# Totals and gate scores in TensorE column groups, and constant products ahead of TensorE's waits

## The reference

```python
x = _layernorm(x + _L0_gnn_ref(x, edge_weight, src, dst, ...))    # message = max over incoming edges
x = _layernorm(x + _L1_gnn_ref(x, edge_attr_64, src, dst, ...))   # edge attention
```

```python
he = edge_features @ edge_fc_W + edge_fc_b
t = relu(einsum('ed,mdf->emf', he, rel_att_W1) + rel_att_b1)          # three relations m
g = sigmoid(einsum('emf,mf->em', t, rel_att_W2) + rel_att_b2)         # gate scores
alpha = _seg_softmax(sum(hs * hd, -1), dst, n)                        # e / sum of e by destination
beta = _seg_softmax(g, dst, n)
h_att = segment_sum(alpha[:, None] * s_att, dst) / kk                 # sums of rows hs, weighted by alpha
h_rel = segment_sum(einsum('em,emf->ef', beta, t_rel), dst) / mm      # and by each of three betas
```

## Time and profile before

| | us |
|---|---|
| timed runs, median of 3 | 2290.52 |
| lowest, highest | 2287.78, 2296.37 |
| span of the profiled execution | 2723.8 |
| TensorE busy in it | 1843.7 (68%) |
| GpSimd busy | 1639.6 (60%) |
| VectorE busy | 1328.7 (49%) |
| ScalarE busy | 1115.3 (41%) |

### The profile page before, as it was taken

One profiled execution on the slowest core, in us unless ns is written; L12 is line 12 of the kernel. 1 busy time (PEld: TensorE's weight loads), 2 busy tenths in 40 slices (PEclk: granted clock), 3 DMA queues, 4 the chain that ended last, 5 costly groups with the idle time before them and its releaser, 6 DMA issues. The chain is left out here.

```text
span 2723.8 us, 43235 instructions
## 1 busy us (share of the span) xinstructions
PE 1843.7 (68%) x9891; PEld 1146.6 (42%) x9891; DVE 1328.7 (49%) x5220; ACT 1115.3 (41%) x3305; POOL 1639.6 (60%) x1705
## 2 busy tenths in 40 slices
PE   4577777677767777655666766676776776766665
PEld 3122222222222222114355655565665665655565
DVE  3454555554444444324535544544544545445459
ACT  1233333333333333333544444444444444444448
POOL 3666666666767777646455655555565655555525
PEclk7689888888889888876867777777777777777788
DMA  8433333333333333323311221221112221211113
GB/s 228 144 120 124 109 116 118 125 109 109 121 109 114 101 123 110 124 80 87 116 46 47 54 51 48 52 51 49 51 51 50 53 52 49 52 48 50 49 44 119
DMA packets 115983, 235.04 MB, mean 86 GB/s; under 512 B 32909, under 2 KB 68230, under 8 KB 106422
## 3 DMA queue, kind: packets, MB, share of 16 engines
q0 software_dynamic: 52832, 109.39, 16.3%
q1 hardware_dynamic: 56522, 97.21, 9.7%
q10 hardware_dynamic: 6540, 27.42, 2.9%
HBM read 166.01 MB, written 67.89 MB: 86 GB/s over the span
## 5 line engine op out<-in xcount | busy, mean ns | idle before, releaser
L463 POOL DMA_INDIRECT d_region<-d_h,d_region x784 | 747.8, 954 | 534.2 <-issue 221.1
L209 POOL DMA_INDIRECT acc<-d_src_product,b_region x784 | 779.4, 994 | 378.6 <-issue 225.5
L651 PE MATMUL banks<-acc,b_region 64*128 64x512 f32 x1176 | 351.8, 706 | 213.9 <-ACT acc L756 99.4
L859 DVE SCALAR_TENSOR_TENSOR acc<-b_region,acc 128x128 f32<-128x128 f32 x784 | 271.4, 346 | 433.6 <-DMA acc<-d_src_product,b_region 416.8
L1577 DVE TENSOR_TENSOR acc<-acc,banks 128x160 f32 x784 | 252.5, 322 | 318.6 <-remote 124.0
L1376 PE MATMUL banks<-d_region 128*128 128x128 f32 x1568 | 306.0, 357 | 4.1 <-issue 3.8
L1379 PE MATMUL banks<-d_region,pick 128*128 128x128 f32 x1568 | 294.1, 346 | 11.6 <-issue 11.2
L651 PEld LDWEIGHTS banks<-acc,b_region 64*128 64x128 f32 x1176 | 109.8, 211 | 429.7 <-issue 188.3
L1379 PEld LDWEIGHTS banks<-d_region,pick 128*128 128x128 f32 x1568 | 277.4, 262 | 13.6 <-issue 13.4
L1376 PEld LDWEIGHTS banks<-d_region 128*128 128x128 f32 x1568 | 271.2, 260 | 10.3 <-issue 5.3
L870 DVE SCALAR_TENSOR_TENSOR acc<-acc,b_region 128x128 f32<-128x128 f32 x784 | 270.1, 345 | 7.5 <-remote 5.2
(11 more groups left out here) (261 smaller groups left out, 2450.3 us busy)
## 6 DMA issues: line engine op xcount, KB each, us to landing
d_runs<-acc SPq DMA_DIRECT2D x48, 1024.0 KB
acc<-ea ACTq DMA_DIRECT2D x25, 1024.0 KB
acc<-d_src_product,b_region POOLq DMA_INDIRECT x784
d_region<-d_h,d_region POOLq DMA_INDIRECT x784
d_region<-d_rel SPq DMA_DIRECT2D x49, 256.0 KB
hT<-xT SPq DMA_DIRECT2D x7, 448.0 KB, 6.9
d_src_product<-acc SPq DMA_DIRECT2D x7, 448.0 KB, 3.7
acc<-xrow SPq DMA_DIRECT2D x1, 3136.0 KB
```

Source lines behind the costliest of these rows:

```text
L209: pool.indirect_dma_start(self.rows[:, s, j, :], None, d["B"], bass.IndirectOffsetOnAxis(self.idx[:, k:k + 1], 0)).then_inc(self.gathered[ ...
L463: pool.indirect_dma_start(rows[:, s, :], None, table, bass.IndirectOffsetOnAxis(idx[:, s:s + 1], 0)).then_inc(gathered[q], 16)
L651: last = nc.tensor.matmul(bank[4 + n % 2 * 2 + h][:, :], wf[h * DE:(h + 1) * DE, m * P:(m + 1) * P], ea[h * DE:(h + 1) * DE, u % (2 * UC), ...
L859: nc.vector.scalar_tensor_tensor(rows[:, s, j, :], wwb, wgt[:, k:k + 1], rows[:, s, j, :], ALU.mult, ALU.add).then_inc(ch, 1)
```

## The change

Three things are changed. The totals become four products with a 32-column stationary of ones (`one`, one column read 32 times), each into 32 partitions of its own: total k now stands in partitions 32k to 32k + 31. The rescale therefore covers 32 partitions, and the last phase takes one of each 32 rows with a product in place of a transpose. The gate scores of relation m go to partitions 32m and 32m + 1, so that three column groups take part instead of two, and the two halves accumulate. And `idle_products` puts products of constants (128x128 bf16 stationary, 256 bf16 columns) into PSUM space that is free by then, ahead of a wait: four in `mlp` before its third relation and four in `dots`, in units whose bank 0 is not in use; two ahead of each of the five steps of the second pass, where the wait that frees the output now stands first.

```diff
+def idle_products(nc, t, to, n):
+    halves = t["ident"].bitcast(BF16)
+    for _ in range(n):
+        nc.tensor.matmul(to, halves[:, 0:P], halves[:, 0:2 * P], start=True, stop=True)
...
+PARTS_END = PART_DVE + PART_STEP * (NC4 - 1) + 6
+IDLE_RUNS, IDLE_EDGES = 4, 2
...
-        wf, w2m = ca(M * P), ca(M * W)
+        wf, w2m = ca(M * P), ca(M * (W + 1))
...
+            def fill(u):
+                if 2 * u < SHIFT_AT - 2 or 2 * u > PARTS_END + 4:
+                    idle_products(nc, t, bank[0][:, 0:2 * P], IDLE_RUNS)
             def mlp(u):
                 pe.wait_ge(eld[u // UC % 2], 16 * (u // UC // 2 + 1))
                 for m in range(M):
                     n = M * u + m
+                    if m == 2:
+                        fill(u)
                     if n >= 2:
                         pe.wait_ge(ra, n - 1)
...
             def dots(u):
+                fill(u)
                 pe.wait_ge(ra, 3 * (u + 1))
                 if u:
                     pe.wait_ge(gc, u)
-                for m in range(M):
-                    for h in range(2):
-                        last = nc.tensor.matmul(bank[3][h * W:(h + 1) * W, :], w2m[:, m * W:(m + 1) * W],
-                                                rt[u % 2][m][:, h * G4:(h + 1) * G4], start=(m == 0), stop=(m == M - 1))
+                for h in range(2):
+                    for m in range(M):
+                        col = m * (W + 1) + 1 - h
+                        last = nc.tensor.matmul(bank[3][m * W:(m + 1) * W, :], w2m[:, col:col + W],
+                                                rt[u % 2][m][:, h * G4:(h + 1) * G4], start=(h == 0), stop=(h == 1))
...
+                if g == PARTS_END:
+                    pe.wait_ge(h2d, NC4)
...
-                    act.dma_start(to[h], gout[u % 2][h * W:h * W + M, :].rearrange("m (t e) -> m t e", t=GJ)
+                    act.dma_start(to[h], gout[u % 2][h:h + (M - 1) * W + 1:W, :].rearrange("m (t e) -> m t e", t=GJ)
...
-                    nc.scalar.activation(gout[u % 2][0:2 * W, :], bank[3][0:2 * W, :], ACT.Copy).then_inc(gc, 1)
+                    nc.scalar.activation(gout[u % 2][0:M * W, :], bank[3][0:M * W, :], ACT.Copy).then_inc(gc, 1)
...
+            def fill(to):
+                idle_products(nc, t, to[:, 0:2 * P], IDLE_EDGES)
             def turn_rows(it, q):
                 s = q % NG
+                pe.wait_ge(hc, it * NG + (q - 1 + 1 + CREDIT))
+                fill(TURNED)
                 pe.wait_ge(gat[s], it * 64 + 64 * lap(q))
-                pe.wait_ge(hc, it * NG + (q - 1 + 1 + CREDIT))
...
             def sums(it, q):
                 s = q % NG
+                pe.wait_ge(ad, it * (NG * GJ) + (q - 2 + 1 + CREDIT) * GJ)
+                fill(bank[5 + q % 2 * 2])
                 pe.wait_ge(wt, it * NG + (q + 1 + CREDIT))
                 pe.wait_ge(bw, it * NG + (q + 1 + CREDIT))
-                pe.wait_ge(ad, it * (NG * GJ) + (q - 2 + 1 + CREDIT) * GJ)
...
                 for k in range(1 + M):
-                    last = nc.tensor.matmul(Z[q % 2], pick[:, M - k:M - k + P], wts[q % 2][:, :, k, :],
-                                            start=(k == 0), stop=(k == M))
+                    last = nc.tensor.matmul(Z[q % 2][k * W:(k + 1) * W, :], one[:, 0:1].to_broadcast([P, W]),
+                                            wts[q % 2][:, :, k, :], start=True, stop=True)
...
-                w = acc[0:1, 4, bass.ds(base[0], 1)]
-                nc.scalar.activation(w, w, ACT.Copy, scale=fac[q % 4][0:1, :]).then_inc(res, 1)
+                w = acc[0:W, 4, bass.ds(base[0], 1)]
+                nc.scalar.activation(w, w, ACT.Copy, scale=fac[q % 4][0:W, :]).then_inc(res, 1)
...
-                    last = nc.tensor.transpose(to[:, K * b:K * (b + 1)], acc[0:K, 4, b * P:(b + 1) * P], ident[0:K, 0:K])
+                    last = nc.tensor.matmul(to[:, K * b:K * (b + 1)], acc[:, 4, b * P:(b + 1) * P], ident[:, 0:P:W],
+                                            start=True, stop=True)
```

More of the change, by code:

```diff
@@ L118, in tensors @@
     t["ident"], t["shift"] = t["shift_ident"][:, 1:1 + P], t["shift_ident"][:, 0:P]
-    t["pick"] = sb("pick", [P, P + M])
+    t["one"] = sb("one", [P, 1])
     t["iota_w"] = sb("iota_w", [P, W])
@@ L255, in _ @@
             c.add(nc.gpsimd.memset(ones, 1.0))
-            c.add(nc.gpsimd.memset(t["pick"][:, :], 0.0))
+            c.add(nc.gpsimd.memset(t["one"][:, :], 1.0))
             c.wait()
@@ L270, in _ @@
                                  allow_small_or_imprecise_dtypes=True))
-            c.add(nc.gpsimd.memset(t["pick"][:, M:M + 1], 1.0))
-            assert c.n == 11
+            assert c.n == 10
             pool.wait_ge(stt, 16)
@@ L337, in _ @@
             c.add(nc.vector.memset(kcum[:, 0:1], 0.0))
-            dve.wait_ge(cst, 11)
+            dve.wait_ge(cst, 10)
             c.add(nc.vector.tensor_tensor_scan(kcum[:, 1:TC], ones[:, 0:TC - 1], km[:, 0:TC - 1], 0.0,
@@ L383, in _ @@
         def _(pe):
-            pe.wait_ge(cst, 11)
+            pe.wait_ge(cst, 10)
             def product(c):
@@ L822, in _ @@
             c.add(nc.vector.tensor_copy(wf, bank[0][:, 0:M * P]))
-            c.add(nc.vector.tensor_copy(w2m[:, 0:M * W:W + 1], w2))
+            c.add(nc.vector.tensor_copy(w2m[:, 1:M * (W + 1):W + 1], w2))
             c.link(nc.vector.tensor_tensor(bf, bank[1][:, 0:M], b1, ALU.add))
@@ L1249, in phase_edges @@
         TURNED, SCORES, WEIGHTS, BOUNDS = bank[0], bank[1], bank[2], bank[3]
-        ident, pick = t["ident"], t["pick"]
+        ident, one = t["ident"], t["one"]
         acc = t["acc"]
@@ L1348, in scores @@
             def scores(it, q):
+                pe.wait_ge(mn, it * NG + (q - 1 + 1 + CREDIT))
+                fill(SCORES)
                 pe.wait_ge(hc, it * NG + (q + 1 + CREDIT))
                 pe.wait_ge(wn, it * NG + (q + 1 + CREDIT))
-                pe.wait_ge(mn, it * NG + (q - 1 + 1 + CREDIT))
                 for j in range(GJ):
@@ L1357, in spread @@
             def spread(it, q):
+                pe.wait_ge(rf, it * NG + (q - 1 + 1 + CREDIT))
+                fill(BOUNDS)
                 pe.wait_ge(mn, it * NG + (q + 1 + CREDIT))
                 pe.wait_ge(sl, it * NG + (q + 1 + CREDIT))
-                pe.wait_ge(rf, it * NG + (q - 1 + 1 + CREDIT))
                 nc.tensor.matmul(BOUNDS[:, 0:8], vals[q % 2][:, 8:9].to_broadcast([P, P]), sel[q % 2][:, 0:8],
@@ L1365, in turn_weights @@
             def turn_weights(it, q):
+                pe.wait_ge(wt, it * NG + (q - 1 + 1 + CREDIT))
+                fill(WEIGHTS)
                 pe.wait_ge(ex, it * NG + (q + 1 + CREDIT))
-                pe.wait_ge(wt, it * NG + (q - 1 + 1 + CREDIT))
                 nc.tensor.transpose(WEIGHTS[:, 0:P], PT[q % 2], ident[:, :]).then_inc(pt, 1)
```

## The result

The time rose: 2311.26 us median (2308.61 to 2313.79) against 2289.15 (2287.20 to 2296.37) for the kernel before in the same runs, ratio 1.0101, 95% interval 1.008 to 1.0122. That is 22 us slower, where the prediction had 7 us faster and a range that ended at 2310.

The account below looks back on a forecast made before the run. Pool's gather pace was taken to bound both passes: profiled 2723.8 us less 434 of waits gave 2290; -13 for residual waits and +6 for the tail gave 2283 us, its own range 2257 to 2303, overall 2200 to 2310.

Parts of the forecast that it names:

- Pool paces both passes: Both gather passes: Pool starts a gather every 1.25 us, 4.99 us a group of four, and other engines keep up.
- The 434 us: Pool's idle time in the profiled passes beyond its fixed gaps, read mostly as a cost of being profiled.
- Totals, gate scores, fills, clock: TensorE in the passes: totals 0.43 us, gate scores 1.85, a group 3.85 with fills, second-pass clock above 0.9.
- The -13 for Pool's residual waits: Gather passes in timed runs: Pool still waits 0 to 72 us, 26 taken, half of it TensorE's and gone.
- The tail: Last phase: 49 transposes from 4 rows become two-pass fp32 products from 128 rows; +6 us, bounds +3 to +13.5.
- Pool's cover: Both passes: TensorE's work with fills stays under Pool's 4.99 us a group and 9.98 a unit, so fills cost nothing.
- TensorE was not on the path: Rival for the passes: TensorE is on the path, so its shorter work shows; 2210 us, range 2160 to 2270, chance 0.27.
- The clock does not rise: Rival: granted clock stays at 0.76 and 0.87, Pool's waits stay, only the tail shows; 2296 us, chance 0.09.
- The fills hold TensorE back: Rival, second pass: fills add 0.95 us to each group at half clock, 37 groups; 2331 us, chance 0.14.
- The prediction's signs of being wrong: Timed runs falling by more than 30 us, or Pool waiting more often for TensorE (L1345 or L1379).

Follow-up runs that it names:

- the run of the tail alone: Kernel before with one edit: the 49 turned totals as fp32 products from 128 rows instead of transposes from 4 rows; 2307.12 us, ratio 1.0078.
- the reordering: Kernel after with VectorE's reference chain (two scans and a minimum) moved ahead of the gate weights, no instruction added; 2298.09 us.
- (7): Gate weights' one-hot table moved from SBUF to PSUM: kernel before 2273.05 us, kernel after (one fill fewer) 2284.35, the latter with totals turned from four rows 2271.67.

## Why the prediction was wrong

**Pool paces both passes: right.** After, Pool starts a gather every 1.25 us (median) in both passes and waits some 8 and 0 us beyond its gap. The 434 us were that one profile's and no timed run has them.

**Totals, gate scores, fills, clock: right, and worth nothing.** Totals 0.43 us as taken from the scores' row, gate scores 1.92 (1.85 taken), a group 5.21 - 1.39 = 3.82 us of TensorE's own (3.85 taken), clock 0.98. Pool's 5 us covers TensorE's work, as the prediction said; once tail and shared input are mended, the change and the kernel before lie at 2271.67 and 2273.05.

**The -13 for Pool's residual waits: wrong.** I allowed 0 to 72 us and took a third, half of it recovered. The second profile of before shows some 7 us in the first pass and none in the second. There was nothing to recover.

**The tail: mechanism right, size wrong.** Taken +6, bounds +3 to +13.5; measured +11.6 in the trace of after, and +18 by the run of the tail alone. I took a value near the low end because the moving side has four columns rather than 128. Here a pass takes 112 ns at full clock against 62 for the old four-row transpose, near the 0.118 us that I had as a middle bound. The loads are busy as long as the passes (13.86 of 13.90 us), which points at the load of a 128-row stationary; rows, passes and kind of product were not varied apart. And the upper bound was too low, because at half clock a pass is 213 ns (I had 171 from a block of products that ran only partly at half clock), and this train of passes falls to half clock on the way, where the prediction let it run at one clock. The Trainium skill (TensorE: Matmul & The Clock Gate, LDWEIGHTS) has P / 1.2 ns for a load of P columns whatever its rows, by estimate 107 for 128 columns: for 128 rows the trace agrees (112), for four it does not (62 with the product). The prediction set the page aside on the second number, and would have done better to keep it for the first.

**The step that was missing: the price of a gather.** The prediction used Pool's 0.94 us as fixed, looked at the other engines only for whether they keep up, and so put the fills under Pool's cover at nothing. They cost the second pass 11.4 us, because what they changed was the cover: a gather went from 967 to 982 ns. The earlier trace rows had means of 994 and 954 against 0.94 in the earlier trace rows, and I did not ask what made the difference. The answer, VectorE's instructions with two SBUF inputs, makes the pace of the bound engine depend on where VectorE's work falls within a gather. The fills change that: at a steady clock 118 of 196 gate weights start 100 to 300 ns ahead of a gather (39 before), and such gathers take 1214 ns (100 to 200 ns ahead) and 1132 ns (200 to 300). That a steady clock is what gathers them in one place is argued from these counts, not shown: no run has the clock without the fills (without them it was 0.76 to 0.88). That the place of the gate weights decides is shown by the reordering, and that the second SBUF input is the cause by the runs of (7). Added up, the 13 us of waits that were not there, 5.6 of tail and 11.4 of gathers are 30 us, where the time missed the forecast by 28.

**Rivals.** TensorE was not on the path (2210 was far off). "The clock does not rise" (2296) was wrong in its premise, though its "the tail alone shows" was half of what came. "The fills hold TensorE back" had the right part of the change and the right sign, but the wrong engine: it priced groups at half clock on TensorE, and the loss came through Pool. The prediction's signs of being wrong were a fall by more than 30 us and more waits of Pool's for TensorE; neither came, and a rise without such waits was not among them.

## What to carry to other kernels

When one engine sets the pace and waits for nobody, read the spread of its own instructions: here the mean above the common value was another engine's work, an instruction of VectorE with two SBUF inputs, and one operand moved to PSUM gave 0.8% where speeding up TensorE gave nothing. A part that no other engine covers is better priced by its number of passes at the rows' price, at both clocks, than by how little moves through it: here 98 passes at 112 and 213 ns give 11 to 21 us, and the turned totals took 15.7 (after) and 17.6 (the tail alone). Before the sum, take a second profile where the first is longer than the timed runs: its idle times and its durations both belong to another schedule. And set a stage's length beside the time of the execution that it was read from, not beside the median.

## What the runs showed of the hardware

- A gather that Pool starts while VectorE runs an instruction with two SBUF inputs ends 0.816 to 0.817 us (median) after that instruction, where the instruction has more than 0.14 us left; with one of the gate weights' inputs in PSUM it takes its 0.944 us. Gate weights that start while a gather is running are not held: they take 559 to 600 ns wherever in the gather they start, in the kernel after. In the first pass the two instructions of the running maximum (L878, L889) go with long gathers in the same way: 26.0 of its 28.7 us over 944 ns lie in gathers that start during them. Taking their second input away was not tried.
- With 32 to 48 records added to a loop of VectorE's its way back rose from 0.26 to 2.8 to 2.9 us a round.
- A chain of fp32 passes with 128 rows of weights and four moving columns took 112 ns a pass and fell from full to half clock, 213 ns a pass, 2.6 and 4.8 us after its start, although TensorE had no idle time in it.
